# Softmax of a windowed attention: negated maximum as the bias of eight small exponentials, and another order of the instructions

## The reference, cut to what matters

```
sim  = einsum('bhwie,bhwje->bhwij', bq, bk2) * QK_SCALE
sim  = where(mask, -finfo.max, sim)
attn = softmax(sim, -1)
out  = einsum('bhwij,bhwje->bhwie', attn, bv2)
x = attn_layer(shift_tokens(x), ...) + x
x = ffn_layer(shift_tokens(x), ...) + x        # layernorm, W1, a * gelu(gate), W2
```

## Time and profile before

| | |
|---|---|
| median of 3 runs | 1641.66 us |
| profiled execution, its own time | 1641.48 us |
| its span, first to last instruction | 1639.7 us |
| mean granted TensorE clock | 0.992 |
| TensorE busy | 1575.6 us, 96% |
| VectorE busy | 1418.0 us, 86% |
| GpSimd busy | 1233.6 us, 75% |
| ScalarE busy | 1113.4 us, 68% |
| exponential, 128x512 | 192 times, 631 ns each |
| maximum / subtraction, 128x512 | 192 times each, 686 and 692 ns |
| loads of the Exp table / of the Gelu table, L750 / L813 | 47 / 48 times, 1283 ns |

### The profile page before, as it was taken

How to read it: one execution, slowest core, us unless ns; L and a number is a source line. 1 busy time by engine, 2 the same in 40 slices (tenths; PEclk the granted TensorE clock), 3 DMA queues, 4 the chain that set the end, 5 groups by cost and what they waited for, 6 DMA issues and landing times.

```text
span 1639.7 us, 75430 instructions
## 1 busy us (share of the span) xinstructions
PE 1575.6 (96%) x31996; PEld 1314.5 (80%) x31996; DVE 1418.0 (86%) x2750; ACT 1113.4 (68%) x1989; POOL 1233.6 (75%) x1200
## 2 busy tenths in 40 slices
PE   6889999999999999999999999999999999999997
PEld 3577888888888888888888888788888878888885
DVE  5798988898899889889988988998889889888963
ACT  4356667766776777676777767776676676667764
POOL 2677877887787878777887777787778887877851
PEclk9899999999999999999999999999999999999998
DMA  3232223333223333322333322333323333322231
GB/s 113 65 73 69 69 69 96 78 84 83 69 69 80 92 79 78 74 70 68 99 75 85 80 69 67 95 80 79 84 66 73 80 92 77 84 71 69 68 100 51
DMA packets 111326, 127.96 MB, mean 78 GB/s; under 512 B 52112, under 2 KB 57744, under 8 KB 110736
## 3 DMA queue, kind: packets, MB, share of 16 engines
q1 hardware_dynamic: 110992, 123.13, 29.8%
HBM read 20.27 MB, written 2.10 MB: 14 GB/s over the span
## 4 chain that ended last, share of the span: by engine, by line
PE 69%; DVE 11%; ACT 10%; issue 6%; SPq 1%; POOL 1%; DMA 1%; POOLq 0%; DVEq 0%; ACTq 0%
PE F L548 10%; PE O L654 10%; PE VTb L569 7%; PE S L605 7%; PE QKb L519 7%; PE F L638 4%; PE QKb L521 4%; PE QKb L520 4%; PE S L617 4%; DVE t L912 3%; ACT L813 3%; PE S L519 2%; PE S L521 2%; DVE mx L923 2%; PE S L520 2%
## 5 line engine op out<-in xcount | busy, mean ns | idle before, releaser
L1087 POOL TENSOR_TENSOR t<-t 128x512 f32<-128x512 f32 x384 | 492.6, 1283 | 188.6 <-DVE t L912 175.4
L1062 POOL TENSOR_TENSOR t<-t,rn 128x512 f32<-128x512 f32 x384 | 402.1, 1047 | 137.2 <-DVE rn L976 137.1
L912 DVE TENSOR_TENSOR t<-QKb,table 128x1024 f32<-128x1024 f32 x384 | 468.7, 1221 | 38.1 <-ACT sq L742 35.0
L742 ACT ACTIVATE sq<-QKb 128x512 f32<-128x512 f32 x384 | 231.7, 603 | 266.1 <-PE QKb L521 266.1
L654 PEld LDWEIGHTS O<-PT,V 64*64 64x64 f32 x12288 | 198.3, 134 | 58.2 <-issue 57.4
L654 PE MATMUL O<-PT,V 64*64 64x32 f32 x12288 | 218.3, 220 | 16.4 <-DVE rn L976 15.9
L936 DVE TENSOR_REDUCE ss<-sq 128x16 f32<-128x1024 f32 x192 | 232.0, 1209 | 0.0
L569 PE MATMUL VTb<-cst,t 128*128 128x128 f32 x1536 | 230.3, 272 | 0.9 <-ACT QT L759 0.7
L548 PEld LDWEIGHTS F<-wo_sb,OT 128*128 128x128 f32 x1536 | 200.2, 191 | 16.6
L1080 POOL TENSOR_TENSOR E<-E,rs 128x512 f32<-128x512 f32 x192 | 200.6, 1045 | 13.3 <-DVE rs L947 13.3
L569 PEld LDWEIGHTS VTb<-cst,t 128*128 128x128 f32 x1536 | 185.3, 141 | 30.9 <-issue 5.4
(11 more groups left out here) (142 smaller groups left out, 2775.4 us busy)
## 6 DMA issues: line engine op xcount, KB each, us to landing
V<-v_tok SPq DMA_DIRECT2D x1440, 64.0 KB, 2.0
w_raw<-in_wqkv SPq DMA_DIRECT2D x36, 256.0 KB, 3.2
wo_sb<-in_wo SPq DMA_DIRECT2D x6, 512.0 KB, 3.9
xs<-xm SPq DMA_DIRECT2D x48, 64.0 KB
xs<-xm SPq DMA_DIRECT2D x48, 63.5 KB
w_sb<-in_w SPq DMA_DIRECT2D x6, 341.0 KB, 4.5
w_sb<-in_w SPq DMA_DIRECT2D x6, 192.0 KB, 3.6
V<-in_x SPq DMA_DIRECT2D x4, 256.0 KB, 3.5
```

The source lines that it names most:

```text
L742: act.activation(sq[:, v % 4, :], QK_ps, ACT.Square).then_inc(sq_done, 1)
L912: dve.tensor_tensor(t12[:, v:9 + v % 4:8 + v % 4 - v, :].rearrange("p c (h d) -> p c h d", h=8), QK_ps.rearrange("p (h d) -> p h d", h=8). ...
L1062: pool.tensor_tensor(w, w, rn[:, vv // 4, 8 * (vv % 4):8 * (vv % 4 + 1)].unsqueeze(2) .to_broadcast([P, 8, DH]), ALU.mult).then_inc(qk_nor ...
L1087: pool.tensor_tensor(w, w, t12[:, 8 + v % 4, :].rearrange("p (h c d) -> p h c d", h=8, c=2)[:, :, ::-1, :], ALU.add).then_inc(add_done, 1)
```

## The change

VectorE takes only the maximum, negated, into `nmx`. ScalarE reads the scores from PSUM and does eight exponentials of 128x64, each with its column of `nmx` as bias; between them nothing is signalled, and the last one raises `exp_done`. `sub_done` is gone; what waited for the subtraction (V and PT on TensorE) waits for `exp_done`. The mask product stays.

The order of the pieces inside a slot is rewritten on every engine:
- TensorE: QK, W1's third chunk (slot 1), WO, x transposes (now slot 6), xn transposes (now slot 7), transposes, PV, S, V, W2, PT, W1's first two chunks.
- ScalarE: exponentials, square, third Gelu, transposes' copy, PV's copy, x staging, first two Gelus, weight rounding, V's copy, affine, PT's copy.
- VectorE: sum with x, sums of squares, gate products, t12, end of the block, sum and reciprocal, x's low half, maximum, layernorm statistics, Newton.
- GpSimd: the division by the sum one slot earlier (lag 12) and last in its slot.

```diff
-L_S, L_EXP, L_NORM, L_PT, L_PV = 11, 12, 13, 14, 16
-F_WO, F_MID, F_SH, F_ST, F_NM, F_XT, F_AFF = 21, 24, 25, 27, 28, 30, 30
+L_S, L_EXP, L_NORM, L_PT, L_PV = 11, 12, 12, 14, 16
+F_WO, F_MID, F_SH, F_ST, F_NM, F_XT, F_AFF = 21, 24, 25, 27, 28, 31, 31
-TX = 4
+TX = 6
...
# VectorE
-                        dve.tensor_reduce(mv_, Sv, AX_X, ALU.max).then_inc(max_done, 1)
-                        wait(dve, max_done, a + 1)
-                        wait(dve, pt_ready, a - 3)
...
-                        dve.tensor_tensor(E[:, k, :].rearrange("p (c b k) -> p c b k", c=4, b=2), Sv,
-                                          mv_.unsqueeze(3).to_broadcast([P, 2, 4, KEYS]),
-                                          ALU.subtract).then_inc(sub_done, 1)
+                        wait(dve, exp_done, a - 3)
+                        dve.tensor_reduce(nmx[:, k, :].rearrange("p (b c) -> p b c", b=2), Sv, AX_X, ALU.max,
+                                          negate=True).then_inc(max_done, 1)
...
# ScalarE, now first in the slot
-                        wait(act, sub_done, a + 1)
-                        act.activation(E[:, k, :], E[:, k, :], ACT.Exp).then_inc(exp_done, 1)
+                        wait(act, max_done, a + 1)
+                        wait(act, pt_ready, a - 3)
...
+                        for c in range(4):
+                            for b in range(2):
+                                i = 2 * c + b
+                                ex = act.activation(E[:, k, KEYS * i:KEYS * (i + 1)], S2[:, b, KEYS * c:KEYS * (c + 1)],
+                                                    ACT.Exp, bias=nmx[:, k, 4 * b + c:4 * b + c + 1])
+                        ex.then_inc(exp_done, 1)
...
# TensorE, V
-                        wait(pe, sub_done, s_units(s, v))
+                        wait(pe, exp_done, s_units(s, v))
# TensorE, PT
-                        wait(pe, sub_done, upto(a + 2, QUADS))
+                        wait(pe, exp_done, s_units(s, v))
# VectorE, table of a new layer
+                    wait(dve, t12_done, s * SLOTS)
```

More of the change, by code:

```diff
@@ L534, in step @@
                         project(QK_ps, par, tile, QK_COLS[2 * half + kind]).then_inc(qk_ready, 1)
+                    f, pr = batch(s, par, v, F_HID)
+                    if f is not None:
+                        ff_w1(f, pr, [2])
                     for k in range(QPS):
@@ L552, in step @@
                                 mm.then_inc(wo_ready, 1)
+                    if v == TX and live(s + 1, STEPS):
+                        wait(pe, ff_final, s + 2 - B)
+                        wait(pe, ff_final, begun(s, v, F_W2))
+                        wait(pe, xn_done, begun(s, v, F_XT))
+                        for t in range(NT):
+                            mm = pe.transpose(BANK_TX[:, P * t:P * (t + 1)], xt[:, (s + 1) % B, t, :], ident)
+                        mm.then_inc(tx_ready, 1)
                     f, pr = batch(s, par, v, F_XT)
@@ L581, in step @@
[L581 to L609, removed]
@@ L621, in step @@
[L621 to L640, removed]
@@ new lines, in step @@
+                    u, vv, st, pr = unit(s, par, v, L_V)
+                    if live(u, UNITS) and vv % 2 == 0:
+                        c = vv // 2
+                        if c % 2 == 0 and st % B == 0:
+                            wait(pe, lo_done[4 + c // 2], st // B + 1)
+                        wait(pe, v_evac, v_units(st, vv, 0) - 1)
+                        wait(pe, exp_done, s_units(s, v))
+                        project(V_ps, pr, c % 2, V_COLS[c // 2]).then_inc(v_ready, 1)
+                    f, pr = batch(s, par, v, F_W2)
@@ new lines, in step @@
+                    if f is not None:
+                        if f % B == 0:
+                            wait(pe, in_w2, (f // B + 1) * 16)
+                        wait(pe, hid_done, (f + 1) * NCH)
+                        for t in range(NT):
+                            for r_ in range(NCH):
+                                mm = pe.matmul(BANK_W2[:, D * t:D * (t + 1)], hid[:, r_, P * t:P * (t + 1)], w2_sb[:, r_, :],
+                                               start=(r_ == 0), stop=(r_ == NCH - 1))
+                        mm.then_inc(w2_ready, 1)
@@ new lines, in step @@
+                    a, k, st, pr = quad(s, par, v, L_PT)
+                    if live(a, QUADS):
+                        wait(pe, p_norm, a + 1)
+                        wait(pe, exp_done, s_units(s, v))
+                        wait(pe, pt_evac, a)
+                        for ct in range(4):
+                            mm = pe.transpose(PT_ps[:, P * ct:P * (ct + 1)], E[:, k, P * ct:P * (ct + 1)], ident)
+                        mm.then_inc(pt_ready, 1)
+                    f, pr = batch(s, par, v, F_W1)
@@ L672, in ff_w1 @@
+                    if f is not None:
+                        if f % B == 0:
+                            wait(pe, in_w1, (f // B + 1) * 16)
+                        wait(pe, xn_done, f + 1)
+                        wait(pe, mid_done, begun(s, v, F_WO))
+                        wait(pe, x_low, staged(s, v))
+                        ff_w1(f, pr, [0, 1])
+                    recurrence(in_fill(s, v, 1))
             def ff_w1(f, par, chunks):
@@ L742, in step @@
                         act.activation(sq[:, v % 4, :], QK_ps, ACT.Square).then_inc(sq_done, 1)
[L743 to L748, removed]
-                        wait(act, sub_done, a + 1)
-                        act.activation(E[:, k, :], E[:, k, :], ACT.Exp).then_inc(exp_done, 1)
+                    f, pr = batch(s, par, v, F_HID)
+                    if f is not None:
+                        gelus(f, pr, [2])
                     u, vv, st, pr = unit(s, par, v, L_TR)
@@ L904, in step @@
                                           ALU.add).then_inc(mid_done, 1)
+                    u, vv, st, pr = unit(s, par, v, L_SS)
+                    if live(u, UNITS) and vv % 2 == 0:
+                        wait(dve, sq_done, u + 2)
+                        dve.tensor_reduce(ss[:, vv // 4, 8 * (vv % 4):8 * (vv % 4) + 16],
+                                          sq[:, vv % 4:vv % 4 + 2, :].rearrange("p a (h d) -> p (a h) d", h=8),
+                                          AX_X, ALU.add).then_inc(ss_done, 1)
+                    f, pr = batch(s, par, v, F_HID)
+                    if f is not None:
+                        hidden(f, pr, [0, 1])
+                    recurrence(in_fill(s, v, 0))
+                    f, pr = batch(s, par, v, F_W2)
+                    if f is not None:
+                        hidden(f, pr, [2])
                     if live(g, UNITS):
@@ L947, in step @@
                         dve.reciprocal(rs[:, k, :], sm[:, k, :]).then_inc(rs_done, 1)
+                    if v == TX and live(s + 1, STEPS):
+                        stage_low(BANK_TX[:, 0:N], 1 - par, 2 * (s + 1))
+                    if s * SLOTS + v == MIXED:
+                        mix(range(EARLY))
+                    a, k, st, pr = quad(s, par, v, L_S)
+                    if live(a, QUADS):
+                        wait(dve, s_ready, a + 1)
+                        Sv = S2[:, :, 0:4 * KEYS].rearrange("p b (c k) -> p b c k", k=KEYS)
+                        wait(dve, exp_done, a - 3)
+                        dve.tensor_reduce(nmx[:, k, :].rearrange("p (b c) -> p b c", b=2), Sv, AX_X, ALU.max,
+                                          negate=True).then_inc(max_done, 1)
                     f, pr = batch(s, par, v, F_ST)
```

130 lines of the change are left out of this document (57 added, 73 removed).

## The result

Before: 1641.26 us (1639.34 to 1642.63, four runs). After: **1731.44 us** (1728.33 to 1737.73, four runs). The ratio is 1.055, with a 95% interval of 1.0535 to 1.0572: slower, as predicted, and inside the range, but 31 us above the 1700. The profiled execution, the longest of the four, took 1737.73 us with a span of 1735.9, against 1641.48 and 1639.7 before: 96.2 us more span to explain (the medians differ by 90.2), of which the forecast had 59.5.

The account below looks back on a forecast made before the run. TensorE was taken as the bound. Per step -0.41 + 1.31 + 0.17 + 0.20, with 0.06 for small margins, gave +1.33; over 44 steps plus 1 that is 59.5 on 1641.48 us: 1700, range 1664 to 1748.

Parts of the forecast that it names:

- Part 1: VectorE: the subtraction goes, 0.61 us to the next start, 192 times; maximum to Newton becomes 0.60 us.
- Part 2: TensorE's new order: PV waits for Newton 1.31 us in slot 2, the main term, and 0.17 in slot 6.
- the old 0.41: TensorE's wait per step before PV of slot 2 for Newton in the kernel before, 0.41 us, expected to go.
- Part 3: ScalarE: eight 64-column exponentials take 1.85 us instead of one of 0.63; the extra 1.2 us is covered.
- rival B: ScalarE becomes the bound: eight exponentials take 2.5 us, QK of slots 3, 5, 7 waits; 1766 us, chance 0.13.
- QK of odd slots waiting for t12: In the profile after, one of two signs that would show rival B; the other was an exponential over 0.35 us.
- only 0.3 us: Margin by which TensorE's even-slot work covers ScalarE's 1.2 us extra; in slot 2 the Exp table reload uses it up.
- Part 4: Rest of the order: V's DMAs about a microsecond later cost nothing; t12 of slot 1 adds 0.2 us per step.
- I add 0.2: Slot 1: t12 ends some 0.3 us after S, moving QK of slot 2 and Newton; 0.2 us per step.
- In the fill ... gains and loses about equally; the drain adds 1: Ends of the run: steps 1 to 3 gain and lose about equally, the drain adds 1 us.
- C: Smaller loss: only PV's wait in slot 2 shows (+0.90), 11.5 us of t12 waits are absorbed; 1670 us, chance 0.17.
- D: VectorE reaches Newton before TensorE needs it, within 1.33 us of S; 1623 us, or 1612; chance 0.05.

Follow-up runs that it names:

- order_only: The changed kernel's order with the softmax of the kernel before (maximum, subtraction, one 128x512 exponential): 1815.28 us, ratio 1.1085.
- a_sh24: The changed kernel with the shifted-x DMAs one slot earlier in SyncE's queue, ahead of V's DMAs of slot 0: 1697.43 us, ratio 1.037.
- sh24_newton: a_sh24 with Newton of slot 1 moved to the start of its slot on VectorE: 1709.62 us, ratio 1.0429.
- one_exp: The changed kernel with one 128x512 exponential from PSUM, one bias column, for the eight (softmax not the reference's): 1718.52 us, ratio 1.050.
- softmax_only: The order of the kernel before with the changed kernel's softmax (negated maximum, eight exponentials with bias): 2175.36 us, ratio 1.327.
- sh24_one: a_sh24 with one exponential from PSUM for the eight (softmax not the reference's): 1690.93 us, ratio 1.032.
- b_newton: The kernel before with Newton of slot 1 at the start of its slot on VectorE, nothing else: 1714.03 us, ratio 1.0468.
- b_wo: The kernel before with WO pieces in slots 2, 5, 6, 7, W1's first chunks ahead of V, wo's load and shifted-x DMAs one slot earlier: 1731.24 us, ratio 1.0558.

## Why the prediction was right in its sign and 31 us short

**Part 1** held: the pitch from maximum to Newton is 0.61 (forecast 0.60), Newton 1.79, PV 0.15 behind it. order_only shows the subtraction's worth in that chain: 0.75 a step and place, near the 0.72 by which maximum and Newton have moved together (1.33 to 0.61).

**Part 2** held, its main term too large: 1.10 a step for 1.31. Part of it was already taken upstream: QK of slot 2 starts 0.35 late for t12, and what TensorE waits there it needs not wait at PV. Slots 2 (PV and QK) sum to 1.45 against the forecast's 1.51. Slot 6 gave 0.23 for 0.17, and the old 0.41 went.

**Part 3** held. The form that had no row now has one, from the page's costliest groups (busy us, mean ns, idle before):

```profile
L748 ACT ACTIVATE E<-S,nmx 128x64 f32<-128x64 f32 x1536 | 336.1, 330 | 152.3 <-DVE nmx L951 151.6
```

330 ns for one (forecast 0.31) and 1.75 us for eight in a row (forecast 1.85). The Gelu was the right neighbour. QK of slots 3 and 7 waits only 0.03 and 0.07 a step, so rival B, the exponentials as the bound, did not occur. One of its two signs did, "QK of odd slots waiting for t12", but at slot 5 alone and for the DMA, as a_sh24 shows: the sign could not tell the two causes apart. And the cover of "only 0.3 us" was as thin as said: with Newton out of the way (sh24_newton) V of slot 2 waits 23.7 us and QK of slot 3 22.9.

The Trainium skill (ScalarE: Activation LUTs, What ACT_TABLE_LOAD costs) would give an estimated 333 ns for one, which agrees with the 330, and with its overlap of 93 ns an estimated 2.01 us for eight; the trace has 1.75, so the measurement decides for more overlap, (8 x 330 - 1750)/7 = 127 ns.

**Part 4 is the step that failed.** It said "V's DMAs on SP's queue are issued about a microsecond later, four slots before PV reads them: nothing." V's copy was delayed by 1.6 us, and PV did not mind: its weight loads wait 2.5 us in all for V's DMAs. What I did not ask is what stands *behind* V's DMAs in that queue: the three DMAs of the shifted x, 4.8 us to issue. Their reader on VectorE has at the same time moved a microsecond forward: it started 14.6 us after W1 before (360.97) and would start 13.6 after it now (380.36 less the 1.27), of which 0.61 is the subtraction that is gone. So the DMAs come 1.6 later and are wanted 1.0 earlier; as a wait of only 1.27 came of it, an estimated 1.3 us of slack had stood there before. The new wait of QK of slot 5 is 0.59 a step, and a_sh24, which moves only these DMAs, runs in 1697.43, 29 to 34 us less. In the same part, "I add 0.2" for t12 of slot 1 was 0.35.

**The ends.** "In the fill ... gains and loses about equally; the drain adds 1" was wrong by 16 us in all. The lead-in grew by 7.5. With one exponential for eight it is 1.9 shorter (160.5 to 158.6 in one_exp, 159.0 to 157.1 under a_sh24), and 1.5 shorter with the earlier DMAs; Each half alone has a longer lead-in than both together, 165.5 in order_only and 176.9 in softmax_only, so how much the order carries was not separated. The last stretch grew by 9.1; a_sh24 takes 3.7 of that (108.7 to 105.0) and sh24_one another 3.8 (101.2). The rest, 1.6, is open.

**The sum.** With the DMAs in time it comes near: 1697 for 1700. That agreement is partly luck. In a_sh24 the step is 33.29, +1.03 for the forecast's +1.33, so 43 steps cost 44.4 us where I had 58.5, and the ends cost 11.4 (lead-in 6.0, last stretch 5.4) where I had 1. Together they are the 55.8 us by which its span exceeds that of before.

**Rivals.** B fell by the size of the exponentials. C (only PV's wait, t12's absorbed) fell: the waits for t12 grew from the earlier trace rows's 11.5 us to 45.9. D's condition, Newton ending within 1.33 us of S, was not met: Newton alone takes 1.79 to 1.81 in the kernels before and after, order_only, b_newton and b_wo.

## What to carry to other kernels

When a step is delayed on one engine, follow the DMA queue that waits for it to its end, not only to the transfer that the step feeds: SyncE issues its DMAs one after the other, so the delay is handed to whatever is behind, and that reader may just have moved forward. When the wait that a trace names is removed, ask which chain was about to end next; here a second chain stood 0.4 us behind the first (V of slot 2 and QK of slot 3 waited 1.05 once the 1.45 of PV and QK of slot 2 were gone), so each cure alone did little or harm and only both showed the gain. And the price of an operation is also its place: the kernel with the same eight exponentials is 90 us above the one before in an order that starts them right after the maximum, and 536 in one that puts a waiting Square ahead.

## What the hardware showed that I had not expected

Eight ScalarE activations of 64 columns with different bias columns overlap well: one every 0.20 us, where one alone takes 0.33.

The granted clock of TensorE followed its waiting only in part. In the change itself, with waits of up to 2.0 us at PV, it stayed at its upper level (2.4 GHz) in every 40 us window from 360 to 560 us, and the mean of the span was 0.989. In order_only, with up to 2.7 there, it was 0.970, and in softmax_only, with up to 3.9 at V, 0.90, in single windows 0.83. In the two windows of softmax_only quoted above TensorE was busy for the same 32.67 of 40 us, once at 0.83 with 520 instructions and once at 1.00 with 692, so the same busy time is not the same work. What decides between them was not tested. A forecast that adds up waits alone is too low once they reach this size.

The three shifted-x DMAs stand in SyncE's queue for 4.8 us, of which L433, the smallest (half rows of one partition), has 3.3 on both sides of the change, where the other two have 0.7 to 0.8. Why was not tried; it is most of what made the queue's order matter.
